# Router bias and gate read into all 128 partitions by DMA, instead of by GpSimd's broadcast over partitions

## The reference, cut to what matters

```python
# x: (4, 256, 128), ctx: (4, 64, 128)
x = x + attn(layernorm(x))          # 16 heads of 8, causal within groups of 32 tokens, q and k RMS-normed
x = x + xattn(layernorm(x), ctx)    # 16 heads of 64 over 64 context rows:
                                    #   (softmax(q k^T) v @ w_out + b_out) * tanh(gate[0])
x = x + ffn(layernorm(x))           # 16 experts, best 4 in the best 2 of 4 groups, and 2 shared experts:
                                    #   scores = sigmoid(x @ router_w.T);  s = scores + bias  (used to choose)
```

## Time and profile before

| | |
|---|---|
| median of 3 runs | 235.35 us |
| lowest, highest | 234.19, 235.88 us |
| profiled execution: span from first to last instruction | 232.5 us |
| median of the runs less that span | 2.85 us |
| PE busy | 195.2 us (84%) |
| DVE, ACT, POOL busy | 156.4, 96.4, 88.7 us |

### The profile page before, as it was taken

How to read it: one execution, slowest core, us unless ns; L and a number is a source line. 1 busy time by engine, 2 the same in 40 slices (tenths; PEclk the granted TensorE clock), 3 DMA queues, 4 the chain that set the end, 5 groups by cost and what they waited for, 6 DMA issues and landing times.

```text
span 232.5 us, 5290 instructions
## 1 busy us (share of the span) xinstructions
PE 195.2 (84%) x1803; PEld 155.7 (67%) x1803; DVE 156.4 (67%) x410; ACT 96.4 (41%) x235; POOL 88.7 (38%) x175
## 2 busy tenths in 40 slices
PE   5780088888877899899999796889999999999991
PEld 5550065656655567776668774777988888888891
DVE  3640055645656348658888977999877878787883
ACT  2420256776776655645554535222222323232320
POOL 4530262456544377626665531422223322420000
PEclk9976559999999999999999997999999999999998
DMA  4966000000000002000000000000110010000002
GB/s 92 357 188 180 0 0 4 4 1 3 3 3 3 0 16 79 0 3 0 0 1 3 0 0 0 24 27 23 34 38 23 23 43 2 0 0 0 1 0 90
DMA packets 10667, 7.36 MB, mean 32 GB/s; under 512 B 1413, under 2 KB 9878, under 8 KB 10518
## 3 DMA queue, kind: packets, MB, share of 16 engines
q1 hardware_dynamic: 10646, 7.09, 10.5%
HBM read 6.56 MB, written 0.52 MB: 30 GB/s over the span
## 4 chain that ended last, share of the span: by engine, by line
PE 53%; ACT 11%; POOL 11%; issue 11%; DVE 11%; DMA 1%; SPq 0%; DVEq 0%; POOLq 0%; ACTq 0%
PE bank L1306 11%; PE wide L1140 6%; PE bank L1169 6%; POOL kbd L446 4%; PE wide L1191 3%; PE wide L1194 3%; PE wide L1192 3%; PE wide L1196 3%; PE wide L1195 3%; PE wide L1193 3%; PE bank L1154 2%; ACT k L590 2%; ACT v L590 2%; POOL rqk L466 2%; DVE act L968 2%
## 5 line engine op out<-in xcount | busy, mean ns | idle before, releaser
L695 ACT ACTIVATE sil<-wide 128x512 f32<-128x512 f32 x36 | 21.5, 599 | 60.1 <-PE wide L1193 60.1
L984 DVE SCALAR_TENSOR_TENSOR x<-bank,combine,x 128x128 f32<-128x128 f32 x128 | 35.9, 345 | 8.9 <-PE bank L1306 8.3
L1306 PEld LDWEIGHTS bank<-dn_w,act 128*128 128x128 f32 x256 | 33.2, 191 | 2.5
L1306 PE MATMUL bank<-dn_w,act 128*128 (+1 forms) x256 | 33.4, 275 | 0.0
L471 POOL TENSOR_TENSOR gu_hi<-gu_w,zero_col 128x256 fp32r<-128x256 f32 x18 | 11.1, 614 | 47.5 <-PE wide L1196 47.5
L968 DVE TENSOR_TENSOR act<-sil,wide 128x512 f32<-128x512 f32 x36 | 24.7, 687 | 4.2 <-ACT sil L695 1.3
L1191 PE MATMUL wide<-x3hi,gu_lo 128*128 128x512 f32 x36 | 17.7, 492 | 2.3 <-DVE act L968 1.8
L446 POOL TENSOR_TENSOR kbd<-qkT,hmask 128x512 f32<-128x512 f32 x8 | 10.6, 1330 | 23.4 <-ACT qkT L553 23.4
L1169 PE MATMUL bank<-vo_fold,p2T 128*128 128x128 f32 x128 | 17.6, 282 | 0.0
L1169 PEld LDWEIGHTS bank<-vo_fold,p2T 128*128 128x128 f32 x128 | 15.7, 193 | 1.0
L1140 PE MATMUL wide<-qk_fold,xn2T 128*128 128x512 f32 x32 | 15.3, 601 | 0.6 <-ACT qk_fold L594 0.4
(11 more groups left out here) (155 smaller groups left out, 420.0 us busy)
## 6 DMA issues: line engine op xcount, KB each, us to landing
wkv_sb<-in_L_xattn_w_kv_dram SPq DMA_DIRECT2D x1, 1024.0 KB, 6.2
gu_w<-in_L_ffn_gate_w_dram SPq DMA_DIRECT2D x16, 64.0 KB, 1.7
gu_w<-in_L_ffn_up_w_dram SPq DMA_DIRECT2D x16, 64.0 KB, 1.9
x<-in_x_dram SPq DMA_DIRECT2D x8, 64.0 KB, 4.2
wq_sb<-in_L_xattn_w_q_dram SPq DMA_DIRECT2D x1, 512.0 KB, 3.9
wout_sb<-in_L_xattn_w_out_dram SPq DMA_DIRECT2D x1, 512.0 KB, 4.9
out_dram<-x SPq DMA_DIRECT2D x8, 64.0 KB, 1.6
wqkv_sb<-in_L_attn_w_qkv_dram SPq DMA_DIRECT2D x1, 192.0 KB, 2.6
```

Source lines behind the costliest of these rows:

```text
L695: sc.activation(sil[:, j % 2, :], bank[j % 2], ACT.Silu).then_inc(sil_s, 1)
L984: dve.scalar_tensor_tensor(out=x[:, t, :], in0=bank[4 + (j + 2) % 4][:, m * D:(m + 1) * D], scalar=combine[:, t, bass.ds(e, 1)], in1=x[:, ...
L1306: last = pe.matmul(bank[4 + (j + 2) % 4][:, m * D:(m + 1) * D], act[:, j % 4, m * P:(m + 1) * P], dn_w[:, bass.ds(n, 1), :].rearrange("p o ...
```

## The change

`router_bias` and `gate` no longer go into `row`; each is read by its own DMA straight into its columns of `rowb` in all 128 partitions (the source pattern has a step of zero over the partitions). POOL's `partition_broadcast` and its wait are gone. `row` keeps `b_out` alone. The readers of `rowb` wait for 32 (two transfers) in place of 1, and the router's DVE part gets that wait too. The columns of `rowb` that held a copy of `b_out` are written no more; nobody read them.

```diff
-        row = sb("row", [1, D + E + 1])
+        row = sb("row", [1, D])
@@ sync (SP)
-            sp.dma_start(row[:, 0:D], b_out.rearrange("(o d) -> o d", o=1)).then_inc(row_l, 16)
-            sp.dma_start(row[:, D:D + E], router_bias.rearrange("(o d) -> o d", o=1)).then_inc(row_l, 16)
-            sp.dma_start(row[:, D + E:D + E + 1], gate.rearrange("(o d) -> o d", o=1)).then_inc(row_l, 16)
+            sp.dma_start(row[:, :], b_out.rearrange("(o d) -> o d", o=1)).then_inc(row_l, 16)
+            sp.dma_start(rowb[:, D:D + E], router_bias.partition_broadcast(P)).then_inc(rowb_r, 16)
+            sp.dma_start(rowb[:, D + E:D + E + 1], gate.partition_broadcast(P)).then_inc(rowb_r, 16)
@@ gpsimd (POOL), late_constants
-                pool.wait_ge(row_l, 48)
-                pool.partition_broadcast(rowb[:, :], row[:, :], P).then_inc(rowb_r, 1)
@@ gpsimd (POOL), step 2
                     pool.wait_ge(tg_r, 1)
-                    pool.tensor_scalar(bias_out[:, :], row[:, 0:D], tgate[0:1, :], None, ALU.mult).then_inc(bo_r, 1)
+                    pool.wait_ge(row_l, 16)
+                    pool.tensor_scalar(bias_out[:, :], row[:, :], tgate[0:1, :], None, ALU.mult).then_inc(bo_r, 1)
@@ scalar (ACT), gate_tanh
-                sc.wait_ge(rowb_r, 1)
+                sc.wait_ge(rowb_r, 32)
@@ vector (DVE), group_scores
                 dve.wait_ge(late_r, 2)
+                dve.wait_ge(rowb_r, 32)
```

## The result

The changed kernel takes **222.42 us** (median; 220.92 to 224.54), the kernel before 235.28 us in the same comparison (234.19 to 235.88). The ratio is 0.9458, with a 95% interval of 0.9405 to 0.951: 5.4% faster. One of the four runs, the one of 224.54 us, counts as a slow one; without it the median is 222.13 us. The profiled execution's span went from 232.5 to 220.4 us, 12.1 us less; its own time was 222.13 us. The forecast was 222.2 us and a span of 219.4.

A forecast was written before the change was run, and what follows sets the result against it. The first stage was taken to hang on POOL's gaps around its broadcast. The stall's 11.85 us plus 1.26 us of clock made 13.1 us, taking 235.35 to 222.2 us; the 8-in-10 range was 220.7 to 225.0.

The forecast's parts named there:

- The stall, 11.85 us: Step 1: without POOL's broadcast and the gaps around it, ACT's copies of kv start 11.85 us earlier.
- That both gaps are the broadcast's: POOL, step 1: the 5.62 us before and 6.97 us after the broadcast are code exchanged out and back; both go.
- The rival that the second gap would stay: POOL's next instruction owes the 6.97 us whatever ran before; about 229.2 us, chance 5%.
- The clock in step 2, 1.26 us: Without the long idle PE keeps 2.4 GHz, so qkn to qkT of step 2 takes 2.51 us, not 3.77.
- The idle that stays is that of the steps from 36 us on, which kept the full clock.: Steps 1 and 2: remaining idle is a few tenths per wait, as in later steps; reason for taking the full 1.26 us.
- The DMAs at no cost: The gate lands by 13.0 us, before ACT's tanh needs it, with at least 2.5 us of slack; cost 0.
- The price of a late landing: ACT's tanh, step 1: each microsecond past 15.55 us is paid in full; late-landing rival 223 to 227.7 us, chance 12%.
- The median: Whole kernel: forecast span 219.4 us plus 2.85 us between span and median gives 222.2 us.

The follow-up runs named there:

- second profile of the changed kernel: The changed kernel itself, measured once more beside a kernel with 24 added PE transposes: 222.22 us, ratio 0.9456 to the kernel before.
- Two kernels with the same idle time and no fillers: The changed kernel plus a broadcast as POOL's last instruction, 228.24 us; the same plus one tensor_scalar behind it, 222.11 us; neither adds PE transposes.

## Why the prediction was right, point by point

- **The stall, 11.85 us.** Between the `qkT`s of steps 0 and 1 it gained 11.80 (12.08 - 0.28). Right, and for the reason given: ACT's next wait was for L1110. The `ms` came earlier than forecast (14.09 against 14.83) since the whole start ran 0.3 us ahead in this profile and the clock fell 0.3 us later; PE's L1110, mostly at the low clock (1.72 us against 1.22), took most of that back.
- **That both gaps are the broadcast's.** Shown by keeping the broadcast (all of the gain gone), and by two calls in a row and a small one, of one profile each. That POOL exchanges its code in them is argued, from what outlived the program. The rival that the second gap would stay is refuted: no gap is left before `ms`. The page of the Trainium skill (GPSIMD Engine Reference, 2.1 Instruction dispatch) prices a first call at about 6 us; the gaps ahead of the broadcast agree (5.62 to 5.93 us), but half of the cost here, the way back (7.04 to 7.36 us in POOL's timeline), it doesn't name, and the measurement decides.
- **The clock in step 2, 1.26 us.** Measured 1.11 (8.82 to 7.71 us between the `qkT`s). The stretch from `qkn` to `qkT` was 2.51 us, as forecast; the rest, 0.15 us, was lost on POOL, whose `kbd` took 1.54 us instead of 1.04. That the term came out is partly luck: by the table above the low clock cost from next to nothing to 1.3 us of step 2, from profile to profile, and the profile before had the most.
- **"The idle that stays is that of the steps from 36 us on, which kept the full clock."** This step failed. In step 2 PE waited 1.68 us for `p1T`, longer than in the later steps (0.24 in step 3), and the clock fell for step 3: 7.97 us between `qkT`s instead of 6.70, so 1.27 us of the gain were given back. The second profile of the changed kernel has the same fall. Two kernels with the same idle time and no fillers haven't, so the fall isn't owed to that idle time alone. The forecast span was 1.0 us too low: these 1.27, the 0.15 of the point above and 0.05 of the stall, less 0.28 at the start and 0.18 gained behind step 3, where the profile before had a low stretch at 142 us that this one hasn't.
- **The DMAs at no cost.** Right: the gate landed at 11.84 us against at most 13.0 forecast, no wait at the tanh. The rule of the Trainium skill that the prediction names (DMA: Bandwidth & Descriptors, Specifications: below 512 B the DMA engine does a read-modify-write) had no visible price: 128 rows of 4 bytes landed in 5.0 us, where the `x` tiles just ahead took 5.8 to 6.0. The price of a late landing was right too: 7.4 us late cost 6.2 to 8.1, by the measure taken.
- **The median.** 222.42 against 222.2 is closer than the mechanism earned. I put 2.85 us between the profiled span and the median; it was 2.02 (222.42 - 220.4), and between 1.73 and 2.84 in the four runs one by one. So a span 1.0 us too low and a distance 0.83 us too high cancel, which is luck. The profile before was also of a run with a low granted clock (0.944; other runs of that kernel had up to 0.971 and spans down to 231.2 us).

## What to carry to other kernels

On POOL, look for "issue" gaps of several microseconds around an instruction of another kind, and count two of them per excursion, one out and one back; group such calls (a second one behind the first had no gap), or put the excursion with its way back where nobody behind it is waited for. A broadcast of a few values over partitions can be a DMA with a step of zero, if it lands before an in-order engine comes to it. And when a stall goes, look at the granted clock behind it in more than one profile, before and after: here the low clock behind the stall cost from next to nothing to 1.3 us, and in both profiles of the changed kernel a new low stretch came a step later.

## What the runs showed of the hardware that was not expected

- Some state of POOL's, by my reading the code that it holds, outlives the program: a kernel that ended on a broadcast paid 7.98 us before its first `affine_select` in the profiled execution, and 0.48 us when one more instruction stood behind the broadcast.
- The way back is longer than the way out: 7.04 to 7.36 us within a program against 5.62 to 5.93 us, whether one or two calls stood between, of 17 to 145 columns (0.33 to 0.48 us each).
- How soon PE leaves the low level at the start differs between runs: the same 10 filler transposes took 1.25 us in the profile of the changed kernel and 2.25 us in another, and the first step ended 1.4 us later.
- The same wait of PE in step 2 (1.5 to 1.7 us) was followed by a fall to 1.2 GHz in two profiles and not in two others.
